# Two feed-forward blocks trade places in a hand-ordered macaron kernel, with a new order for k, v, q and the FIR

## The reference

```python
x = x + 0.5 * ffn(layernorm(x))       # block A
x = x + attn(layernorm(x))
x = x + 0.5 * ffn(layernorm(x))       # block C, same weights
# ffn: 256 -> 1024, gelu, 1024 -> 256
# attn: q, k, v = silu(4-tap causal conv(x @ W)); beta = sigmoid(x @ Wb)
#   delta rule over chunks of 32 (T = inverse of a unit lower triangular matrix)
#   branches = [FIR3(v), FIR31(v), delta, v], 4 heads of 64
#   gate: mean, rms, max of the branches, the branches themselves and x @ gW1
#         -> gelu -> softmax over the 4 branches, floored
#   o = sum of gated branches, normalised per head, @ Wo
```

## Time and profile before

| | |
|---|---|
| time, median of 2 runs | 1224.95 us (1223.7 to 1226.2) |
| the profiled execution's own time | 1227.37 us |
| its span, first to last instruction | 1225.7 us |
| mean granted TensorE clock | 0.932 |
| busy: PE, DVE, ACT, POOL | 1056.4, 820.9, 549.3, 415.6 us |

### The profile page before, as it was taken

One profiled execution on the slowest core, in us unless ns is written; L12 is line 12 of the kernel. 1 busy time (PEld: TensorE's weight loads), 2 busy tenths in 40 slices (PEclk: granted clock), 3 DMA queues, 4 the chain that ended last, 5 costly groups with the idle time before them and its releaser, 6 DMA issues.

```text
span 1225.7 us, 25639 instructions
## 1 busy us (share of the span) xinstructions
PE 1056.4 (86%) x10348; PEld 784.7 (64%) x10348; DVE 820.9 (67%) x1556; ACT 549.3 (45%) x965; POOL 415.6 (34%) x648
## 2 busy tenths in 40 slices
PE   3778598899988999899988996999988998887838
PEld 2654485378745886488736884478736885477427
DVE  5774267785687767875788666875787667863263
ACT  1154236443374337543475336453475337532322
POOL 7106500671019500681028400681028400870000
PEclk9889699899999999989999999999999999995668
DMA  5040104110040203111040203011040204020000
GB/s 153 1 102 21 34 1 97 25 31 22 18 104 1 53 1 94 28 26 27 19 104 1 52 19 86 18 24 30 18 104 1 52 1 96 9 52 1 1 0 18
DMA packets 82293, 47.45 MB, mean 39 GB/s; under 512 B 57856, under 2 KB 75776, under 8 KB 82176
## 3 DMA queue, kind: packets, MB, share of 16 engines
q1 hardware_dynamic: 82176, 45.82, 16.4%
HBM read 31.12 MB, written 14.68 MB: 37 GB/s over the span
## 4 chain that ended last, share of the span: by engine, by line
PE 57%; DVE 22%; ACT 8%; issue 5%; SPq 3%; POOL 3%; DMA 1%; DVEq 0%; ACTq 0%; POOLq 0%
PE psum L782 12%; PE psum L784 10%; PE psum L783 10%; DVE conv_acc L1363 4%; PE psum L813 4%; DVE arena L1594 3%; PE psum L975 3%; PE psum L960 3%; PE psum L994 2%; PE psum L999 2%; SPq L347 2%; PE psum L1152 2%; ACT arena L582 2%; DVE arena L1596 2%; POOL arena L522 1%
## 5 line engine op out<-in xcount | busy, mean ns | idle before, releaser
L518 POOL TENSOR_TENSOR l_prod<-arena 64x30 f32<-64x30 f32 (+14 forms) x240 | 150.8, 628 | 599.2 <-DMA arena<-l_dram 581.0
L578 ACT ACTIVATE h_f<-psum,b_col 128x512 f32<-128x512 f32 x128 | 88.0, 688 | 216.4 <-PE psum L784 206.4
L522 POOL TENSOR_TENSOR arena<-arena,l_prod 64x30 f32<-64x30 f32 (+14 forms) x240 | 157.3, 655 | 18.8
L782 PE MATMUL psum<-w_hi,h_hi 128*128 128x256 f32 x512 | 152.0, 297 | 9.2 <-DVE h_lo L1343 9.2
L784 PE MATMUL psum<-w_hi,h_lo 128*128 128x256 f32 x512 | 145.2, 284 | 0.0
L783 PE MATMUL psum<-w_lo,h_hi 128*128 128x256 f32 x512 | 145.1, 283 | 0.0
L1081 PE MATMUL psum<-v_shift,fir_w 128*32 128x512 f32 x1152 | 133.6, 604 | 3.6 <-DMA v_shift<-v_dram 3.6
L1363 DVE SCALAR_TENSOR_TENSOR conv_acc<-psum,conv_col,conv_acc 128x511 f32<-128x511 f32 x144 | 107.8, 748 | 33.5 <-ACT conv_acc L603 22.4
L782 PE MATMUL psum<-xt_hi,w_hi 128*128 128x512 f32 x256 | 109.4, 427 | 14.3 <-DVE b_half L1456 7.0
L1342 DVE CAST h_hi<-h_f 128x512 fp32r<-128x512 f32 x128 | 65.3, 510 | 76.6 <-ACT h_f L578 40.1
L782 PEld LDWEIGHTS psum<-w_hi,h_hi 128*128 128x128 f32 x512 | 98.1, 192 | 15.3 <-DVE h_lo L1343 11.1
(11 more groups left out here) (232 smaller groups left out, 2205.6 us busy)
## 6 DMA issues: line engine op xcount, KB each, us to landing
x_in<-in_L_attn_x SPq DMA_DIRECT2D x8, 512.0 KB, 4.0
v_dram<-v_fm SPq DMA_DIRECT2D x8, 512.0 KB, 2.8
v_shift<-v_dram SPq DMA_DIRECT2D x8, 512.0 KB, 5.0
out<-x_tok SPq DMA_DIRECT2D x8, 512.0 KB, 2.9
v_shift<-v_dram SPq DMA_DIRECT2D x8, 511.0 KB, 7.0
v_shift<-v_dram SPq DMA_DIRECT2D x8, 510.0 KB, 9.1
v_shift<-v_dram SPq DMA_DIRECT2D x8, 509.0 KB, 11.6
arena<-in_L_ffn_w SPq DMA_DIRECT2D x2, 1024.0 KB, 7.1
```

The source lines that it names most:

```text
L518: pool.tensor_tensor(prod, l_inv[:, k + 1:, k:k + 1].broadcast_to(shape), l_inv[:, k:k + 1, 0:k].broadcast_to(shape), ALU.mult).then_inc(i ...
L522: pool.tensor_tensor(l_inv[:, k + 1:, 0:k], l_inv[:, k + 1:, 0:k], prod, ALU.add).then_inc(inverted, 1)
L578: act.activation(h_f[:, m % 2, :], bank, ACT.Gelu, bias=b1_col[:, m:m + 1]).then_inc(read, 1)
L782: pe.matmul(dst, a_hi, b_hi, start=first, stop=False, **kw)
```

## The change

Block A moves out of the recurrence, and block C moves into it, one pass later. The recurrence of sequence i is now filled with block C of sequence i - 1 (`upr`, `outr`, the "fill" blocks), and block A of sequence j + 1 is computed in the middle of the pass, two sequences ahead of the recurrence (`upw`, `outw`, the "wide" blocks), with its steps between the slots of the FIR, ahead of the mixture. The first recurrence then has no filler, and it gets a pass of its own kind, `zero`; there are five bodies instead of six. `last` has no block A left to compute; `tail` fills its recurrence with block C of sequence 6 and ends with block C of sequence 7.

The convolutions run in the order k, v, q. The second layer norm is normalised inside `merge`, turned after tiles 2 and 3, and the first half of k is projected inside the last tile step. k is turned and multiplied right after the turned delta output. On VectorE `k_rows`, the statistics and the normalisation of the next block A, and four of the six convolutions stand ahead of `hidden`'s last two. beta is computed in token layout, with 24 products of four columns in place of six of 512 columns and four turns. The three row buffers become a ring that is used by sequence number, so POOL's copy goes, and the input of sequence j + 1 is loaded as soon as the output of sequence i - 1 has been stored from the same buffer. SP sends L out ahead of v, POOL adds its two biases ahead of the inversion.

The diff, cut to tables and orders; of the removed lines, which stand in the kernel above, none is shown again:

```diff
+        FFN_R = [("upr", (2, 3) + (2,) * (KT - 2)), ("outr", (3, 4))]
+        LN2 = [("ln2", (2, 7))]
+        K = [("k", (2, 7)), ("beta", (0,))]
+        GATE = [("gate", (5, 6, 3, 4)), ("dv_t", (1, 0, 1, 0))]
+        GRAM = [("k_t", (2, 7)), ("gram", (0, 1))]
+        V = [("v", (2, 7))]
+        STAT = [("stat", (0,))]
+        Q = [("q", (1, 0)), ("hidden", (2,))]
+        LN1 = [("ln1", (7, 5))]
+        FFN_W = [("upw", (6, 5) * (KT // 2)), ("outw", (3, 4))]
+        LOGIT = [("logit", (7,)), ("logit_t", (7,))]
+        FIR = [("q_t", (1, 0)), ("fir", (7, 2, 1, 0))]
+        MIX = [("mix_t", (5, 6)), ("wo", (3, 4))]
+        V_T = [("v_t", (5, 6)), ("f_t", (7, 2, 1, 0)), ("lhalf", (5, 6)), ("at0", (3, 4))]
         NEXT = [("next", (7, 2))]
+        L_OFF = [("at1", (5, 6)), ("lpair", (1, 0))]
+        LN3 = [("ln3", (7, 2))]
+        first = [("first", (2, 6)), ("upr", (2, 0) * (KT // 2)), ("outr", (3, 4)), ("sums", (5, 1))]
+        recur = [MERGE, RECUR]
+        early = [LN2, K, GATE, GRAM, V, STAT, Q]
+        ORDER = {"head": sum([LN2, K, GRAM, V, Q, LN1, FFN_W, FIR, V_T, L_OFF], first),
+                 "zero": sum(recur + early + [LN1, FFN_W, LOGIT, FIR, MIX, V_T, NEXT, L_OFF], []),
+                 "body": sum(recur + [FFN_R] + early + [LN1, FFN_W, LOGIT, FIR, MIX, V_T, NEXT, L_OFF], []),
+                 "last": sum(recur + [FFN_R] + early + [LOGIT, FIR, MIX, V_T, NEXT, L_OFF], []),
+                 "tail": sum(recur + [FFN_R, GATE, STAT, LOGIT, MIX, LN3, FFN_W], [])}
...
+            def add_bias(seq, n, added):
+                x_seq = rows_of(seq)
+                pool.wait_ge(xn_made[n], (1 if n == 0 else 2) * (seq + 1))
+                for t in range(TILES):
+                    last = pool.tensor_tensor(x_seq[:, t, :], x_seq[:, t, :], b2_half[:, :], ALU.add)
+                last.then_inc(added, 1)
+                pool.wait_ge(added, seq + 1)
...
+                if at.fill:
+                    add_bias(at.i - 1, 2, bias2_added)
+                if at.ahead:
+                    x_ready(pool, at.j + 1)
+                    add_bias(at.j + 1, 0, bias1_added)
...
+                if at.fill:
+                    store_y(at.i - 1)
+                if at.ahead and at.back:
+                    if at.fill:
+                        sp.wait_ge(y_stored, 16 * at.i)
+                    else:
+                        sp.wait_ge(setup_dve, SETUP_DVE)
+                    load_x(at.j + 1)
                 if at.front:
                     j = at.j
+                    sp.wait_ge(l_made, j + 1)
+                    sp.dma_start(l_dram.rearrange("c i u j -> (c i) u j"), l_tok[:, :, :]).then_inc(l_stored, 16)
...
+                    sp.wait_ge(silu_made, 6 * j + 4)
...
+                if at.front:
+                    tap(0)
+                if at.back:
                     stat_square(at, 5)
+                if at.front:
+                    tap(1)
                 if at.back:
                     stat_square(at, 6)
+                    stat_square(at, 7)
+                if at.front:
...
+                if at.back:
+                    for h in range(2):
                         out_of(at, "dv_t", h, dv_fm[h])
+                if at.front:
+                    silu(0)
+                    silu(1)
+                if at.back:
+                    for h in range(2, HEADS):
+                        out_of(at, "dv_t", h, dv_fm[h])
+                if at.front:
+                    for t in range(2):
+                        bank, _ = arrive(act, at, "k_t", t)
...
+                        act.activation(sq[:, t, :], bank, ACT.Square).then_inc(kq_squared, 1)
+                    for t in range(2):
+                        out_of(at, "k_t", t, arena[:, 0, 512 * t:512 * t + 512])
+                    act.wait_ge(nrm_made, j + 1)
+                    act.activation(nrm[:, 0, :], nrm[:, 0, :], ACT.Sqrt).then_inc(kqroot_made, 1)
+                if at.ahead:
+                    root(0, j + 1)
+                if at.front:
+                    tap(2)
                 if at.back:
...
                 if at.front:
                     tap(3)
                     silu(2)
+                    tap(4)
                     silu(3)
+                    tap(5)
+                if at.ahead:
+                    high(at, 0, j + 1, "ln1")
                 if at.back:
                     for h in range(HEADS):
                         gate_gelu(h)
                 if at.front:
+                    out_of(at, "hidden", 0, hid_fm[:, :])
+                def wide_gelu(m):
+                    if at.wide:
+                        gelu(at, 1, at.w, m)
+                if at.front:
+                    wide_gelu(0)
+                    wide_gelu(1)
                 if at.back:
...
                 if at.front:
+                    wide_gelu(2)
+                    silu(4)
+                    silu(5)
                 if at.back:
                     act.wait_ge(lshift_made, i + 1)
                     act.activation(lg[:, :, :], lg[:, :, :], ACT.Exp).then_inc(exp_made, 1)
                 if at.front:
+                    wide_gelu(3)
+                    wide_gelu(4)
...
+                    wide_gelu(5)
+                    wide_gelu(6)
+                    wide_gelu(7)
...
+                    if t == TILES - 1 and at.front:
+                        turn(at, "ln2", 1, lambda n: xn_tok[:, n, P:2 * P])
...
+                elif at.front:
+                    copied(pe, at, "ln2", 0)
+                    copied(pe, at, "ln2", 1)
+                    projection(at, "k", 0, 0)
...
+                if t == TILES - 2 and at.front:
+                    pe.wait_ge(xn_made[1], at.j + 1)
+                    turn(at, "ln2", 0, lambda n: xn_tok[:, n, 0:P])
...
                 for t in range(TILES):
+                    toks = slice(P * t, P * t + P)
+                    for k in range(HALVES):
+                        last = product3(pe, bank[:, 32 * t:32 * t + HEADS], xt_hi[:, k, toks], xt_lo[:, k, toks],
+                                        wb_hi[:, k, 0:HEADS], wb_lo[:, k, 0:HEADS], k == 0, k == HALVES - 1)
                 last.then_inc(full, 1)
...
+                if at.front:
+                    projection(at, "k", 1, 0)
+                if at.back:
+                    gate_f(at, 0)
+                    gate_f(at, 1)
+                if at.front:
+                    beta(at)
                 if at.back:
                     gate_f(at, 2)
                     gate_f(at, 3)
...
                 if at.front:
+                    pe.wait_ge(silu_made, 6 * j + 2)
+                    to_tok(at, "k_t", lambda h: qk_fm[:, h, 0, :])
+                    k_products(at)
                 if at.back:
                     for h in range(HEADS):
                         copied(pe, at, "dv_t", h)
                         gate_d(at, h)
                 if at.front:
                     projection(at, "v", 0, 2)
+                    projection(at, "v", 1, 2)
                 if at.back:
                     pe.wait_ge(max_made, i + 1)
...
                 if at.front:
+                    projection(at, "q", 0, 1)
                 if at.back:
                     pe.wait_ge(stat_made, i + 1)
                     gate_stats(at)
                 if at.front:
                     projection(at, "q", 1, 1)
...
+                if at.ahead:
+                    turn_rows(at, "ln1", xn_made[0], j + 2)
+                    wide(range(0, 8))
...
+                if at.ahead:
+                    wide(range(8, 12))
                 if at.back:
                     copied(pe, at, "logit")
                     turn(at, "logit_t", 0, lambda t: lg_fm[:, P * t:P * t + P])
+                if at.ahead:
+                    wide(range(12, 16))
+                if at.front:
                     pe.wait_ge(silu_made, 6 * j + 6)
                     to_tok(at, "q_t", lambda h: qk_fm[:, h, 1, :])
+                    pe.wait_ge(v_shifted, 64 * j + 64)
+                    firs(at, 0, range(0, 2))
+                if at.ahead:
+                    wide(range(16, 20))
+                if at.front:
+                    firs(at, 0, range(2, 4))
...
+                    attend(at, 0)
+                if at.keep:
+                    turn_rows(at, "next", xn_made[2], 2 * i + 2)
+                if at.front:
+                    attend(at, 1)
+                    off_diagonal(at, "lpair")
...
+                    if at.front:
+                        normalise(1, j, rows_of(j))
...
+                if at.fill:
+                    dve.wait_ge(bias2_added, i)
+                    residual("outr", rows_of(i - 1), rows_of(i - 1), y_made)
                 if at.back:
                     stat_sum(4)
                     delta_out(3)
                 if at.front:
+                    conv(0)
                 if at.back:
                     stat_sum(5)
                     max_of_d(2)
+                if at.front:
+                    conv(1)
+                if at.back:
```

(37 more changed lines are left out.)

456 lines of the change are left out of this document (180 added, 276 removed).

## The result

The changed kernel takes 1283.42 us (median of 2 runs, 1278.6 and 1288.2) against 1224.95: 1.048 times the time before, with a 95% interval of 1.030 to 1.065. A later set of four runs, beside seven of the kernel before, gave 1283.8 and 1.045 (1.039 to 1.052). It is slower, as forecast, but by 58 us instead of 27, and 5 us outside the range. The profiled execution took 1288.2 us, its span is 1286.3.

The account below looks back on a forecast made before the run. TensorE was taken as the bound, busy 126.4 of 135.3 us per body. Head +4, `zero` +1, five bodies +35, `last` -9, tail -4.5 gave +27 on the span of 1225.7, forecast 1252 us, range 1195 to 1278.

Parts of the forecast that it names:

- The mechanism: Steady body: PE's work stays, but PE, in order, meets late results, mostly VectorE's; waits 15.1 us against 8.9 now.
- the chain: Body, steps on VectorE and ScalarE from tile 3's L960 to the first wide gelu: done at 44.1 us.
- The rival of a shorter chain: Body: 35.5 instead of 44 us to first wide gelu; no change (1227), chance 0.35, or faster (1197), 0.17.
- The 30.5 of PE's work: Body: PE's work in us from tile 3's L960 to the third wide "up", waits not counted.
- The waits: Body: PE waits 2.1 at k's turn, 4.4 `gate_stats`, 1.8 `ln1`, 4.2 third "up", 2.6 behind; 15.1 in all.
- the term for the clock in the body: Half clock: one old loss gone, one behind each wait over 4 us; +1.8 us per body, bounds -1.8 and +3.6.
- The head: Pass before the recurrences, 144.3 us: gains a block and `ln1`, 23.5, mostly hidden in idle time; +4, between 0 and +8.4.
- zero: First recurrence pass, without filler, against the old first body of 143.4 us: recurrence 1.2 longer, 144.4, so +1.
- last: Pass after the bodies, 131.6 us: one block less, -22.4, idle time up to some 23; -9 in all.
- Tail: Final pass: recurrence at full clock beside filler, 1.2 us less, products around it shorter too; -4.5, to 121.
- The stalls: Two unexplained PE waits, 8.0 and 6.5 us, near k's small products and v's loads: gone; if back elsewhere, 1267, chance 0.05.
- t_loaded: Rival: this load signal becomes the bound behind `fir_done`, some 3 us per pass, 1270; chance 0.03.

Follow-up runs that it names:

- e7: Changed kernel plus four unused reductions on VectorE ahead of the last two hidden sums; 1307.3 us, ratio 1.062 to the kernel before.
- e2: Changed kernel with LN1's statistics moved into VectorE's idle time and its normalising ahead of v's first convolution; 1264.2 us, ratio 1.027 to the kernel before.
- e1: Changed kernel with q's convolutions moved behind the gate's hidden sums on VectorE; 1267.6 us, ratio 1.028 to the kernel before.
- e3: Changed kernel with two heads' `gate_d` products moved ahead of k's turn; 1286.8 us, ratio 1.045 to the kernel before.
- e8: Changed kernel with q's first projection and the second wide "up" each run three times over, results unchanged; 1272.3 us, ratio 1.034 to the kernel before.
- e5: Changed kernel with e1, e2 and the `lpair` wait moved ahead of y1, all together; 1222.8 us, ratio 0.994 to the kernel before.
- e6: On e5, ScalarE's first wide gelu ahead of the last two gate gelus, VectorE's split of it between q's convolutions; 1213.3 us, ratio 0.986.
- e10: On e6, `beta`'s 24 products over 32 columns instead of 4; 1212.8 us against 1213.3, ratio 0.988 to the kernel before.
- the second profile: The changed kernel run once more with no edit; 1283.8 us.
- e9: On e6, 60 constant products, never read, in the unfilled slots of the first recurrence; 1209.4 us, ratio 0.984 to the kernel before.

## Why the forecast came out as it did

**The mechanism held, and the chain with it.** From the end of tile 3's L1006 (494.0) the steps of the forecast read: first convolution 5.6 (forecast 5.9), second 9.4 (9.8), k's silus 13.9 (13.3), L 20.9 (20.8), clip 28.3 (29.0), `hidden(3)` 41.1 (42.1), third "up" 43.1 (44.1). The rival of a shorter chain named 35.5 against 44 as the point that decides; with 43.1 measured it is dead. (The 30.5 of PE's work that it leans on come to 31.4 when its pieces are added up; 44.1 less the four waits ahead of it, 12.5, gives 31.6. The rival had even less idle time to expect than it says.)

**The waits held, each by its name:** 1.8 at k's turn (2.1), 3.1 at `gate_stats` (4.4), 1.3 at `ln1` (1.8), 3.5 at the third "up" (4.2), and 4.1 at the splits and the pass's end (2.6). Idle time is 14.1 per body, forecast 15.1; that the sum is so near is partly luck, since 1.3 too much at `gate_stats` meets 1.5 too little at the splits and the pass's end. `e7` shows that VectorE's queue causes the third "up"'s wait, `e2` that LN1's statistics and normalising cause that of `gate_stats`, and `e1` that q's convolutions ahead of the hidden sums are some 2 us of the former. `e3` shows that the wait at k's turn isn't an extra: without it PE waits as much longer for the clip.

**The failed step is the term for the clock in the body**, "one behind each wait of over 4: 3.6 - 1.8 = 1.8 more", that is 128.2 us of busy time. It is 131.8. I took the rule from one wait of 1.8 that was followed by half clock and one of 2.8 that wasn't, set the border at 4, which neither of them supports, and found two candidates. No wait in a body reached 4, so by the rule there should have been no loss at all. The losses are 19 in five bodies against 8 before, behind waits of 3.5 and of 2.3 to 2.7 too, while the 3.1 at `gate_stats` in the body shown has none behind it (in two of the other three it has one). So the length of the single wait draws no border, and the term is some 4 us more per body and not 1.8. The upper bound that I gave, +3.6, was about right, and I should have taken a value near it: `e8` shows that the half clock behind two of the waits comes from PE's idling, and `e5` that with three of them shorter the body runs at clock 1.00. Why it falls behind one wait and not behind the next stays open: `e6` waits less than `e5` and has more half clock, and `e10` didn't find the cause. Of the body's +9.6 us in all, some 4 are clock, 4.3 waits (5.9 more than before without the stall's 1.6 per body), and 1 to 1.5 other busy time, about what `beta` takes more, which I had put at no change: "PE waits there anyway". Over five bodies this is 729.2 against 716.

**The head**, +4 forecast, took +14.5, and +9.8 in the second profile. The bounds were 0 and +8.4, and the upper one was nearer again. The 11.0 us ahead of y1 did fall to 1.1. In exchange the head's own front waits at the wide block: 3.1 and 2.5 us for v's convolutions to empty the banks of `hidden` and `ln1`, 2.5 for the low half. I had counted the block as filler for an idle head without running the body's chain through it: PE's idle time in the head fell by 10.9 us (56.6 to 45.7), where the term of +4 counts on 19.5. That is 8.6 of the 10.5 us that it missed by.

**`zero`**, +1 forecast, took +6.6. My row for the recurrence without filler was taken in the tail and ended at the last L960; up to there it holds (35.8). But the pass stays at half clock beyond it, through k's first projection and the last products: 41.7 us at clock 0.55 from y1 to the first product behind the recurrence, where a new body, with filler, takes 38.7 at 1.00. That is 3.0 instead of 1.2. Read as far, the old trace would have shown it: 42.6 in the tail, 38.1 in a body. Of the 5.6 missed, 1.8 are this, 2.6 are the miss of every body, and the rest lies behind the recurrence too. `e9` shows that the clock is the cause: products that nobody reads shorten this stretch by 9 us.

**The other terms:** `last` 126.3 (forecast 122.5), at clock 0.95 where the old one had 0.99: half clock costs 6.3 us in it instead of 1.3. Tail 122.0 (121). The stalls, counted as gone, are: the largest wait of PE for "issue" is 1.3 us, and 2.6 in any run after it. That speaks for the link with k's small products and v's loads, but moving both at once doesn't tell which. The Trainium skill, page "Runtime: NRT & Kernel Launch", section "Instruction fetch mechanics", says that fetching is hidden; no run here tested it. `t_loaded` never bounds a pass: y1 waits 1.1 us for `lpair` in the head and for nothing longer elsewhere.

So, against 1225.7 + 27, the miss of 34 us on the span is 10.5 head, 5.6 `zero`, 13 bodies, 4 `last`, 1 tail. Direction, places and chain were right; each term was mis-sized to the same side. In the bodies, `zero` and `last` that is mostly half clock, which stood in the sum once where it occurs again and again; in the head it is mostly waits that the block brought with it.

The price of function tables stood as read in the earlier trace rows. In the chain's new place ScalarE loads silu's table and starts the activation behind it 1.29 us later:

```profile
505.44 1.28 ACT L621 ACT_TABLE_LOAD   x1
506.73 1.15 ACT L621 ACTIVATE qk_fm<-conv_acc 128x512 f32<-128x512 f32 x2
```

The Trainium skill, page "ScalarE: Activation LUTs", section "What ACT_TABLE_LOAD costs", adds 1.38 us of drain to each; the trace again doesn't show it.

## What to carry to other kernels

- When work trades places on an in-order engine, follow the second engine's queue to each result that the first one needs; fill the queue's idle time first. Here four moves of whole steps on VectorE, ScalarE and PE turned 1.045 times the old time into 0.986 without taking out any work.
- Ask of each wait of TensorE whether half clock follows it, and price that beside the wait. The length of the wait doesn't tell: here 2.3 to 2.7 us at the pass's end had it behind them in every body, 3.1 at `gate_stats` in two of four. Edits that left 12, 18 and 16 losses of half clock one by one left 1 together, so price several waits together and not one by one.
- Read a row of the trace to the end of the step that it prices: in the kernel before, the recurrence without filler is 1.2 us longer up to the last L960 and 4.5 longer at its end.
- A wait that is covered may only move to the next thing that hangs on the same queue (`e3`). Look for where that queue is still late before counting a gain.

## What was not expected of the hardware

TensorE made the kernel faster by doing more: 24 idle products per pass took 11.5 us off, and 60 in the first recurrence shortened it from 42.1 to 33.0 us (clock 0.52 to 1.00). And half clock can begin while PE is busy throughout, with no wait in the trace for 45 us ahead of it (608 us in `e6_gelu_first`); wider products at that place didn't change it.
